# A tabular-model kernel whose selected features are copied two tables at a time, with one transpose group moved ahead of a selection

## What is computed

```python
e = jnp.stack([tbl_0[ids[:, 0]], ..., tbl_25[ids[:, 25]]], axis=1)
combined = jnp.concatenate([dense_features[:, None, :], e], axis=1)
interactions = jnp.einsum('bfd,bgd->bfg', combined, combined)
z = jnp.concatenate([dense_features, interactions[:, _IU0, _IU1]], axis=1)
h = jnp.concatenate([z, r_dense_features], axis=1)
h = jnp.maximum(h @ W_top1 + b_top1, 0.0)
h = jnp.maximum(h @ W_top2 + b_top2, 0.0)
y = h @ W_top3
```

## Time and profile before

| What | Time or share |
|---|---|
| Median of three runs | 527.55 us (525.3 to 530.39) |
| Profiled execution, its own time | 527.54 us |
| Its span in the trace | 525.4 us |
| PE, matmuls | 398.8 us, 76% of the span |
| POOL | 260.7 us, 50% |
| DVE | 204.2 us, 39% |
| ACT | 160.5 us, 31% |
| PE idle before selections, until a copy from `p_sel` (pairs 2 to 7) | 26.4 us in 11 waits |

### The profile page before, as it was taken

How to read it: one execution, slowest core, us unless ns; L and a number is a source line. 1 busy time by engine, 2 the same in 40 slices (tenths; PEclk the granted TensorE clock), 3 DMA queues, 4 the chain that set the end, 5 groups by cost and what they waited for, 6 DMA issues and landing times.

```text
span 525.4 us, 9717 instructions
## 1 busy us (share of the span) xinstructions
PE 398.8 (76%) x3968; PEld 357.2 (68%) x3968; DVE 204.2 (39%) x157; ACT 160.5 (31%) x314; POOL 260.7 (50%) x278
## 2 busy tenths in 40 slices
PE   3641947674697689966897789955897588979997
PEld 2530846564586588955886578945886587868887
DVE  6110935553233434450533434450533532545103
ACT  0000543262222244214422333214421432226330
POOL 6774765645435654555546654565445653540000
PEclk9965877887898779978899679986999778979999
DMA  8981221743313152314414161313414140222031
GB/s 212 260 274 30 86 62 40 174 81 107 131 29 79 41 129 78 72 47 92 118 35 77 45 155 45 66 51 65 144 36 77 40 100 25 47 45 55 3 58 28
DMA packets 66355, 43.88 MB, mean 84 GB/s; under 512 B 51713, under 2 KB 56408, under 8 KB 66204
## 3 DMA queue, kind: packets, MB, share of 16 engines
q1 hardware_dynamic: 56068, 25.48, 20.1%
q0 software_dynamic: 8704, 17.84, 13.3%
q10 hardware_dynamic: 1560, 0.24, 0.3%
HBM read 37.78 MB, written 5.76 MB: 83 GB/s over the span
## 4 chain that ended last, share of the span: by engine, by line
PE 54%; another core or an unknown queue 26%; issue 7%; ACT 7%; DMA 3%; DVE 1%; ACTq 1%; SPq 1%; DVEq 0%
PE p_sel L411 24%; PE p_gram L433 9%; PE p_mlp L454 7%; PE p_turn L369 5%; PE p_mlp L491 3%; ACT feats L603 3%; ACT feats L580 3%; PE p_mlp L448 2%; DMA dense<-in_x_t 2%; PE p_sel L381 2%; ACT prods L618 1%; DMA square<-prods 1%; PE p_mlp L503 1%; DMA pairs_h<-square 1%
## 5 line engine op out<-in xcount | busy, mean ns | idle before, releaser
L341 POOL DMA_INDIRECT rows<-in_table,index x272 | 260.1, 956 | 208.2 <-PE p_turn L369 79.5
L713 DVE TENSOR_TENSOR onehot<-ids_all,p_rows 128x2048 fp32r<-128x2048 int32 x72 | 163.0, 2283 | 156.6 <-PE p_sel L411 83.8
L411 PE MATMUL p_sel<-onehot,high 125*128 125x256 f32 x528 | 153.4, 322 | 41.3 <-ACT feats L603 33.1
L411 PE MATMUL p_sel<-onehot,low 125*128 125x256 f32 x528 | 146.0, 308 | 1.8 <-issue 1.8
L411 PEld LDWEIGHTS p_sel<-onehot,high 125*128 125x128 f32 x528 | 114.9, 218 | 45.8 <-issue 25.6
L411 PEld LDWEIGHTS p_sel<-onehot,low 125*128 125x128 f32 x528 | 115.1, 218 | 3.2 <-issue 2.9
L580 ACT ACTIVATE feats<-p_turn 128x512 f32<-128x512 f32 (+1 forms) x80 | 79.6, 996 | 87.5 <-PE p_turn L369 49.2
L433 PEld LDWEIGHTS p_gram<-feats 128*54 128x54 f32 x2048 | 71.8, 156 | 50.5 <-issue 38.6
L433 PE MATMUL p_gram<-feats 128*54 128x52 f32 x2048 | 80.6, 241 | 33.1 <-ACT feats L580 17.3
L603 ACT ACTIVATE feats<-p_sel 128x128 f32<-128x128 f32 x144 | 44.6, 443 | 112.3 <-remote 65.5
L618 ACT ACTIVATE prods<-p_gram 118x416 f32<-118x416 f32 x64 | 33.4, 522 | 134.0 <-remote 93.7
(11 more groups left out here) (46 smaller groups left out, 124.8 us busy)
## 6 DMA issues: line engine op xcount, KB each, us to landing
ids_all<-in_ids_t SPq DMA_DIRECT2D x25, 256.0 KB, 4.7
square<-prods SPq DMA_DIRECT2D x62, 87.8 KB
rows<-in_table,index POOLq DMA_INDIRECT x272
pairs_h<-square SPq DMA_DIRECT2D x14, 117.0 KB
weights<-in_table SPq DMA_DIRECT2D x3, 448.0 KB
prods<-in_table SPq DMA_DIRECT2D x3, 448.0 KB
ids_all<-in_ids_t SPq DMA_DIRECT2D x1, 1152.0 KB
ids_all<-in_ids_t SPq DMA_DIRECT2D x6, 128.0 KB
```

The lines of the kernel that those rows point to most:

```text
L341: pool.indirect_dma_start(out=rows[a][:, f, :], out_offset=None, in_=tables[f], in_offset=bass.IndirectOffsetOnAxis(ap=index[:, (2 * i + a ...
L411: mm = pe.matmul(p_sel[bank][:, half * PAIR:half * PAIR + PAIR], part[k][0:VP, c, :], hot, start=(c == 0 and part is high), stop=(c == VC ...
L713: nc.vector.tensor_tensor(onehot[k % RING][:, :, :], at, of, ALU.is_equal).then_inc(s_onehot, 1)
```

## The change

Three things change, for pairs 1 to 7. The two tables that share a bank of `p_sel` are placed in reverse (`1 - k % 2`), so that they stand in the order of their places in `feats`, and `keep_held(i, bank)` copies both with one instruction per tile (256 elements in place of twice 128). In pairs 2 to 7, ACT copies held bank 0 ahead of the products of gram bank 3, and held bank 1 right behind them, so both stand ahead of keep 2. And `selections` starts at quad 3 in place of quad 2: PE turns quad 3 directly behind quad 2, then runs selections 4 and 5, turn 4, and selections 6, 7 and 8. ACT's copies of tables 4 to 8 follow the same new order.

```diff
-    start = 1 if second else 2
+    start = 1 if second else 3
...
-    return (k // 2, k % 2) if k < HELD and not first else (k % 2, 0)
+    return (k // 2, 1 - k % 2) if k < HELD and not first else (k % 2, 0)
...
-                if k == 0 and not first:
-
-                    act.wait_ge(s_gram, NG * 2 * i)
...
+            def keep_held(i, bank):
+
+                f = C - 2 - 2 * bank
+                if bank == 0:
+
+                    act.wait_ge(s_gram, NG * 2 * i)
+                act.wait_ge(s_sel, SEL * i + 2 * bank + 2)
+                held = p_sel[bank].rearrange("d (f a j g) -> d f a j g", f=2, a=2, j=4)
+                for a in range(2):
+                    dst = feats[a][:, :, :, f:f + 2].rearrange("d g j f -> d f j g")
+                    ins = nc.scalar.activation(dst, held[:, :, a, :, :], ACT.Copy)
+                ins.then_inc(s_fsel, 2)
...
-                        keep_prods(i - 1, 1, range(NH * q, NH * q + NH))
-                    if not first and q == (0 if second else 1):
-                        for k in range(HELD // 2):
-                            keep_selected(i, k)
+                        keep_prods(i - 1, 1, (NH * q,))
+                        if q == 1:
+                            keep_held(i, 0)
+                        keep_prods(i - 1, 1, (NH * q + 1,))
+                        if q == 1:
+                            keep_held(i, 1)
+                    if second and q == 0:
+                        keep_held(i, 0)
...
-                    if not first and q == (1 if second else 2):
-                        for k in range(HELD // 2, HELD):
-                            keep_selected(i, k)
+                    if second and q == 1:
+                        keep_held(i, 1)
```

## The result

The changed kernel took **551.72 us** (median of 4 runs, 545.35 to 553.76), the kernel before in the same comparison 528.25 us (4 runs, 525.3 to 530.39). The ratio is 1.041, 95% interval 1.030 to 1.052. The forecast of 523.4 us has the wrong sign, and the time lies above the range. The profiled execution took 550.78 us, 23.2 us more than the profiled one of before.

A forecast was written before the change was run, and what follows sets the result against it. No one engine was taken as the bound: PE is kept waiting for answers. From 527.54 us, -2.3 (copies), -4.3 (turn 3) and +2.5 (POOL's queue) sum to -4.1, so 523.4 us; range 517 to 529.5 us.

The forecast's parts named there:

- Held bank 0 ahead of products 3, in fewer instructions: ACT's copies ahead of selection 4: selection 4 starts 0.38 us earlier in each of six pairs, -2.3 us.
- the gate: The moment ACT gets leave to copy the products of gram bank 3; selection 4 was forecast about 1.17 us behind it.
- Turn 3 ahead of selection 4: PE, pairs 2 to 7: turn 3 runs in the idle stretch behind turn 2, -4.3 us, bounds -4.3 and 0.
- POOL's queue: POOL in pairs 2 and 5: gathers become runs of eight, and these pairs give back 1.23 us each, +2.5 us.
- The third rival: Selection 6: ACT hears of selection 4 only behind POOL's run of eight, +12.4 us of waits, 533.3 us; chance 0.10.
- the full 6.6 us of gain: The gain from the copies' place and turn 3 together, with nothing given back.
- SP's store: Store, read-back and layer 1 behind products 3, done about 0.9 us later: taken as 0, bounds 0 and +0.5 us.
- The gate stays where it is behind turn 2,: Assumption that ACT's leave at gram bank 3 does not move; the forecast is wrong if it does.
- The range: The whole kernel's time was expected between 517 and 529.5 us.
- bounds on the copies: ACT's 256-element copies: from -5.0 us in all (128-element cost) to +3.3 us (512-element cost).
- what is given back: Pairs 2 and 5 lose their gain again by becoming like the other pairs, +2.5 us; lower bound 0.

The follow-up runs named there:

- e4: The changed kernel without the gathers of pairs 1 to 7 (rows of pair 0 reused): 405.99 us, ratio 0.774 to the kernel before.
- e2: The kernel before with only turn 3 moved ahead of selection 4, ACT's copies as before: 543.68 us, ratio 1.040.
- e14: The kernel before with turn 3 ahead of selection 4 and POOL's quad 3 of tile 0 waiting for turn 4: 529.31 us, ratio 1.000.
- e9: The changed kernel as it is, timed again on another chip: 548.96 us, ratio 1.032 to the kernel before at 533.78 us.
- e10: The changed kernel with POOL's quad 3 of tile 0 waiting for turn 4, parting quads 2 and 3: 529.94 us, ratio 0.995.
- e11: The kernel before with POOL's quad 2 of tile 0 waiting for turn 3, joining quads 2 and 3: 556.53 us, ratio 1.039.
- e13: The kernel before with POOL's quad 3 of tile 0 waiting for turn 4: 550.84 us, ratio 1.040.
- e5: The changed kernel with POOL's quad 3 of tile 0 waiting for turn 4, where nothing is held: 385.4 us, ratio 1.010 to the kernel before at 380.15.
- e12: The kernel before with only ACT's copies changed, turn 3 still behind selection 4: 546.56 us, ratio 1.028.
- e17: The kernel before with an 8-element iota behind each gather of pairs 1 to 7, POOL waiting for its end: 443.01 us, ratio 1.166.
- e18: The changed kernel with an 8-element iota behind each gather, POOL waiting for its end: 445.36 us, ratio 1.175 to the kernel before.
- e3: The kernel before without the gathers of pairs 1 to 7 (rows of pair 0 reused): 405.15 us, ratio 0.774.

## Why the prediction was wrong, step by step

- *Held bank 0 ahead of products 3, in fewer instructions:* right on the copy and the gate: 673 ns for the copy (675), 1.15 us from the gate to selection 4 in pairs 2 and 3 (1.17). Its -2.3 us as a saving of the whole is not seen, in e4 either.
- *Turn 3 ahead of selection 4:* right in its mechanism: it is directly behind turn 2. Its 4.3 us, as a saving of the whole kernel, are shown nowhere: e2 is 4% slower, e14 no faster.
- *POOL's queue:* **the step that failed.** It took +2.5 us, the price of two pairs becoming like the other three. Measured, the waits behind selection 4 grew by 14.9 us in the five pairs, and PE's late matmuls in pair 5 cost some 4.8 more. Moving POOL alone is worth 19 to 23 us: one wait of POOL is worth 19.0 us between e9 and e10, and 22.8 us between the kernel before and e11. POOL did not get "runs of eight in pairs 2 to 6": it has them in pairs 2 and 4, but one of twelve in pair 3 and of nine in pairs 5 and 6. I had read from the earlier trace rows that answers are held while POOL gathers, and then priced it by the waits of the kernel before, as if the runs would stay where they were. They do not, as e10, e11 and e13 show, each by one wait of POOL. My reading is that an answer held longer lets POOL's next run begin elsewhere, and POOL's own waits for turns grow (79.5 to 112.8 us).
- *The third rival* named the mechanism, ACT hearing of selection 4 only behind POOL's run, and pair 3 now has it at its place. Its +12.4 us for the waits was near the 14.9 measured, though it took pair 3's old 2.76 us as the worst, where the run of twelve made 8.19. Its 533.3 us were too low because it set the full 6.6 us of gain against them, and left out PE's late matmuls and what lies ahead of pair 2. Its evidence against (pairs 4 and 6 answered at once) was two of three cases, too thin for a chance of 0.10.
- *SP's store:* taken at 0, bounds 0 and +0.5, in pair 7 alone. 1.14 us of wait in pair 7; in the loop pairs nothing where answers are held. Where they are not, e5's layer 1 waits 1.1 to 1.7 us a pair and gives all of the gain back. "Several more microseconds lie between" was true only of a kernel with other waits to hide in.
- *The gate stays where it is behind turn 2,* the assumption named last. In pair 3 it did (2.5 us of idle for ACT); in pair 5 ACT got its leave 0.2 us behind the start of turn 2, without a wait for "remote". And the gate is itself a held answer, so no sum taken against it was safe.
- *The range* was made from bounds on the copies and on what is given back, none of which knew that one wait of another engine decides 4%.

**Open:** what in the chip holds PE's answers, and what sets the condition. That PE's own matmuls come late beside a run ("issue") speaks for something wider than semaphores, the supply of PE's instructions for one; no run takes the two apart. The condition is not a matter of the chip as such: the chip of e9 to e12 (before at 533.78 us) was also that of e17 and e18 (before at 379.59). The three sets without POOL stops met one condition, the two with such kernels the other; whether that is chance was not tested. Open too is why e13 loses in the pairs whose runs are short. The change itself was never timed where nothing is held, only with an extra wait of POOL that never stopped it (e5).

## What to carry to other kernels

Where a chain holds a large share of "another core or an unknown queue", find out what holds the answers before costing an edit: one run with the suspect taken away (here 530 to 405 us) says more than any sum of waits. Under such a hold, engines that look independent can come to take turns, and one moved wait cost or gave some 20 us here; try moving the other engine's start first. And time the kernel before in every set: its own time moved from 530 to 380 us between sets, far more than any edit here.

## What the runs showed of the hardware

- PE's answers can reach the other engines late while POOL issues indirect gathers back to back: a wait of 8.19 us beside a run of twelve, and of 23.18 us for ACT beside a run of 34. PE's own matmuls can come late too: 25.2 us of "issue" idle ahead of gram matmuls in the changed kernel, none without gathers (e3). The same kernel with plain transfers of the same bytes takes 407.6 us in place of 531.2.
- The hold is a condition that comes and goes: 380 or 530 us for the same program, on one and the same chip at different times (e9 to e12, e17 and e18); a gather takes 0.96 us in both.
- A stop of POOL behind a gather for a 0.15 us instruction costs 0.27 or 0.83 us of idle on top of it.
- Copies of 128, 256 and 512 fp32 elements a partition into places 432 bytes apart take 443, 673 and 1138 ns, on one line.
